# Causal attention layer: the mask of the second pass as TensorE products on the scores, in place of GpSimd selects on the probabilities

## The reference

```python
q, kk, v = [(layernorm(x) @ W.T + b) split into 16 heads of 8 features]
dot = einsum('bhqd,bhkd->bhqk', q, kk)
dot = where(causal, dot, -inf) / sqrt(128)      # key k counts for query q only if k <= q
attn = softmax(dot, axis=-1)
x = x + einsum('bhqk,bhkd->bhqd', attn, v) @ Wo.T + Wo_b
```

## Time and profile before

| What | Value |
|---|---|
| median of 3 runs | 1955.01 us (1954.34 to 1955.83) |
| the profiled execution's own time | 1949.83 us |
| its span in the profile | 1948.0 us |
| mean granted TensorE clock | 0.952 of full speed |
| PE / DVE / ACT / POOL busy | 85% / 72% / 54% / 28% of the span |

### The profile page before, as it was taken

The page is one execution under the profiler, slowest core; times in us unless marked ns, Lnnn a source line. Parts: engine busy times, 40 slices in busy tenths (PEclk is TensorE's granted clock), DMA queues, the critical chain, the costliest instruction groups (busy, mean ns, idle before and its releaser), DMA issues. The chain is left out here.

```text
span 1948.0 us, 37580 instructions
## 1 busy us (share of the span) xinstructions
PE 1659.1 (85%) x12701; PEld 945.7 (49%) x12781; DVE 1400.6 (72%) x4005; ACT 1046.9 (54%) x2110; POOL 543.9 (28%) x739
## 2 busy tenths in 40 slices
PE   3788888889999989996799999999997867688666
PEld 1344434333333333332467776767675645556444
DVE  6788868788788878881467766766664588665887
ACT  1566666666767776775554445445443454343553
POOL 6566656662333333201100000000002323200232
PEclk9899999999999999998899999999999988899798
DMA  5335333332322112200000000000000000000000
GB/s 96 62 64 104 67 64 51 52 50 41 50 51 50 30 32 40 50 2 1 1 2 2 2 2 2 2 3 2 2 2 1 1 1 0 1 1 1 6 16 22
DMA packets 56698, 49.89 MB, mean 26 GB/s; under 512 B 9220, under 2 KB 54468, under 8 KB 56516
## 3 DMA queue, kind: packets, MB, share of 16 engines
q1 hardware_dynamic: 53692, 46.45, 13.1%
q10 hardware_dynamic: 2824, 1.11, 0.4%
HBM read 7.10 MB, written 2.10 MB: 5 GB/s over the span
## 5 line engine op out<-in xcount | busy, mean ns | idle before, releaser
L515 ACT ACTIVATE at_probs<-ps 128x512 f32<-128x512 f32 (+1 forms) x864 | 458.7, 581 | 219.7 <-PE ps L630 162.8
L774 DVE TENSOR_REDUCE at_M<-ps 128x1 f32<-128x512 f32 x512 | 330.1, 682 | 78.7 <-PE ps L606 77.5
L606 PE MATMUL ps<-at_KS,at_QS 96*128 96x512 bf16 (+3 forms) x1024 | 324.2, 348 | 39.9 <-DMA at_KS<-at_splitk 18.2
L630 PE MATMUL ps<-at_QS,at_KS 128*128 128x512 bf16 x944 | 294.0, 342 | 10.7 <-ACT at_probs L515 10.5
L769 DVE CUSTOM_DVE_ANT_0 at_masked<-ps,at_mask_row 128x384 bf16<-128x384 f32 (+3 forms) x512 | 227.1, 484 | 63.2 <-PE ps L606 61.2
L647 PE MATMUL ps<-at_probs,at_V 128*9 128x512 f32 (+3 forms) x2048 | 228.7, 519 | 26.2 <-POOL at_probs L394 19.2
L606 PEld LDWEIGHTS ps<-at_KS,at_QS 96*128 96x128 bf16 x1024 | 94.4, 99 | 253.0 <-DVE at_M L774 105.8
L394 POOL TENSOR_SCALAR_AFFINE_SELECT at_probs<-at_probs 128x128 f32<-128x128 f32 (+2 forms) x352 | 118.1, 346 | 125.2 <-ACT at_probs L515 119.7
L630 PEld LDWEIGHTS ps<-at_QS,at_KS 128*128 128x128 bf16 x1024 | 97.7, 99 | 101.9 <-ACT at_probs L515 30.6
L856 POOL TENSOR_TENSOR la_rstd<-la_vare,mhalf 128x4 f32<-128x4 f32 x16 | 16.1, 1008 | 420.9 <-DVE la_vare L851 420.9
L1267 DVE SCALAR_TENSOR_TENSOR la_phiq<-ps,la_ezq 128x512 f32<-128x512 f32 x64 | 44.1, 690 | 114.9 <-ACT la_ezq L1118 114.9
(11 more groups left out here) (258 smaller groups left out, 3342.6 us busy)
## 6 DMA issues: line engine op xcount, KB each, us to landing
at_QS<-at_splitq SPq DMA_DIRECT2D x288, 64.0 KB
at_KS<-at_splitk SPq DMA_DIRECT2D x279, 64.0 KB
out<-X SPq DMA_DIRECT2D x8, 256.0 KB, 2.3
at_QS<-at_nmT ACTq DMA_DIRECT2D x64, 8.0 KB
at_KS<-at_splitk ACTq DMA_DIRECT2D x9, 64.0 KB
w_raw<-fp_weights SPq DMA_DIRECT2D x1, 560.0 KB, 6.6
w_wv<-L_attn_a_wv SPq DMA_DIRECT2D x1, 512.0 KB, 8.7
w_wo<-L_attn_a_wo SPq DMA_DIRECT2D x1, 512.0 KB, 5.7
```

The source lines that it names most:

```text
L515: act.activation(v(probs[u % 8][:]), v(src), ACT.Exp, scale=layers[layer(n)]["scale"])\
L606: last = pe.matmul(ps[:, FIRST + U % 3, o * stride:o * stride + width], QS[n % 2][0:SHIFT_AT, h, qt * P:(qt + 1) * P], KS[n % 2][0:SHIFT_A ...
L630: last = pe.matmul(ps[:, SECOND + u % 3, c:c + width], KS[n % 2][:, h, kt * P:(kt + 1) * P], QS[n % 2][:, h, 512 - width:512], start=True, ...
L774: v.tensor_reduce(M[gq % 2][:, heads[0]:heads[-1] + 1, qt], src, AX.X, ALU.max).then_inc(max_free, 1)
```

## The change

For each of the 16 products of a causal quad's second pass, a second product follows on TensorE, onto the first 128 columns of the same scores: identity times `mask_kq`, without start, so that it adds -1e30 to the masked scores before ScalarE reads them. The selects on GpSimd and their semaphore are gone, and `sum_keys` waits for ScalarE in both layers. Everything behind line 278 moves up by up to 11 lines.

```diff
-    probs_masked = sem("probs_masked")
...
-        def clear_future(n, q, gq, i):
-            if not causal[layer(n)]:
-                return
-            _, heads, width, stride = second_of(n)[i]
-            u = seconds(gq) + i
-            diagonal = probs[u % 8][:].rearrange("p (h c) -> p h c", c=stride)[:, 0:len(heads), 0:P]
-            g.wait_ge(scores_free, u + 1)
-            g.affine_select(out=diagonal, in_=diagonal, compare_op=ALU.is_ge, fill=0.0, base=0,
-                            pattern=[[0, len(heads)], [1, P]], channel_multiplier=-1).then_inc(probs_masked, 1)
...
-        walk({"spread": root, "turn": turn, "split": split_part, "clear": clear_stacks, "scores": clear_future,
+        walk({"spread": root, "turn": turn, "split": split_part, "clear": clear_stacks,
...
+                masked = causal[layer(n)]
                 last = pe.matmul(ps[:, SECOND + u % 3, c:c + width], KS[n % 2][:, h, kt * P:(kt + 1) * P],
-                                 QS[n % 2][:, h, 512 - width:512], start=True, stop=True)
+                                 QS[n % 2][:, h, 512 - width:512], start=True, stop=not masked)
+                if masked:
+                    last = pe.matmul(ps[:, SECOND + u % 3, c:c + P], core["ident16"][:], core["mask_kq"][:],
+                                     start=False, stop=True)
...
-            pe.wait_ge(probs_masked if causal[layer(n)] else scores_free, seconds(gq) + last_unit(n, kt) + 1)
+            pe.wait_ge(scores_free, seconds(gq) + last_unit(n, kt) + 1)
```

## The result

The change makes the kernel about 1% faster: 1934.71 us in the median of 5 runs (1933.66 to 1941.19) against 1954.34 for the kernel before beside it (5 runs, 1951.58 to 1955.83), a ratio of 0.9906 [0.9889 to 0.9923]. A second set gave 1934.7 and 0.9908 [0.9888 to 0.9929]. The profiled execution took 1933.66 us, its span 1931.9.

What follows compares the result with a forecast made beforehand. No engine was full: TensorE and VectorE wait for each other in turn, TensorE leading an item's first part, VectorE the second. 16.5 us added less 21.3 removed gave about -5 us: 1955.0 to 1950.0 us, range 1941 to 1960.

Steps and rivals of the forecast that it cites:

- What the products cost: Causal second pass, TensorE: 512 added mask products at 0.056 us each, 278 counting, plus 0.9 us at the start: 16.5 us.
- rival 1: Mask products on TensorE pay their weight loads, about 0.091 us each: 5 us slower, 1960 us; chance 0.15.
- The sums: Second-pass sums on TensorE no longer wait for GpSimd's selects: 2.1 us an item, 14 us saved; bounds 0 and 19.2.
- Rival 2: TensorE then waits for VectorE to free first-pass banks, losing half of the 14 us: 1957 us, no change; chance 0.25.
- The start: First sum of the causal stage, at 63 to 67 us, no longer waits for GpSimd: 3.2 us saved; bounds 0 and 3.7.
- The rotation: GpSimd's rotation steps for items 8 and 9 finish earlier, so TensorE waits less: 3.1 us saved; bounds 1 and 3.3.
- VectorE: VectorE's small instructions collide less with GpSimd on shared ports: 1.0 us saved over the stage; bounds -3 and +4.
- The removal as a whole: Taking 352 selects off GpSimd in the causal second pass saves 14 + 3.2 + 3.1 + 1.0 = 21.3 us.
- The sum, carried to the median: Whole kernel: 16.5 - 21.3 = -4.8, say -5 us, taken from the 1955.0 us median of the runs: 1950.0 us.
- Rival 3: VectorE leads more, only a third of the masks lie on the path: 13 us faster, 1942 us; chance 0.12.

Runs made afterwards that it cites:

- a second set: The changed kernel with each mask product made twice, 512 more products with the output unchanged: 1955.01 us, 0.9992 of the kernel before.
- the kernel with neither: The changed kernel without the 512 mask products and without the selects, so the second pass is unmasked: 1922.22 us, 0.9812 of the kernel before.
- the one-quad kernel: The kernel before with mask products instead of selects only in item 0's first quad (16 products): 1949.87 us, ratio 0.9984.
- the first trace of before: The profiled execution of the unchanged kernel before that the prediction was made from: 1949.8 us, item 10's projection to k at 491.8 us.
- The idle selects: The changed kernel with 352 selects put back at their old places in GpSimd's queue, on scratch tiles nobody reads: 1950.43 us, 0.997 of the kernel before.
- the third trace: Another profiled execution of the kernel before, nothing changed, taken after the prediction: item 10's projection to k at 500.5 us.
- the second trace: A further profiled execution of the kernel before, nothing changed, taken after the prediction: item 10's projection to k at 500.5 us.

## Why the prediction was wrong, step by step

The forecast named the right mechanisms and had their sizes wrong. Its miss of 15 us has two halves. In the very trace that it was made from, the change is worth 13.2 us at item 10 and not 4.8: the removal gave 26.6 where 21.3 was counted, and the products took 13.4 where 16.5 was. And from that trace to the typical execution a further 7 us came, which the last step of the sum put at nothing.

- **What the products cost.** About right. 16.5 us forecast; 11 to 18 measured, and 17 and 20 for a second set. In a steady item 1.9 us, which is the prediction's own count: 36 of them less the 3 before ScalarE's copies, times 0.056, is 1.85. With it fell rival 1: eight products last 0.61 us, not 0.75. The Trainium skill (TensorE: Matmul & The Clock Gate, "Back-to-back issue gap") would have 0.081 us for each pair of load and product; the trace does not agree, at 0.056.
- **The sums.** Right in a steady item: 2.1 us forecast for the removal; without products the steps from item to item were 2.15 us shorter, and with them the item is 45.3 us. Over the stage it was taken a little low: no sum waits in the kernel with neither, so all of the 16.0 us are gone where 14 were counted. Rival 2, that the waits move to VectorE's banks, fell: TensorE waited 1.6 us for them in the kernel after, and 7.6 before.
- **The start.** Undersized. I took TensorE's own idle time, 3.2 us; it measured 5.0 in the kernel without products, and 4.4 net in the one-quad kernel where 2.3 was forecast. The bound of 3.7 did not hold it. Most of the further 1.8 us is the clock's: behind its wait, the first trace of before has this (67.1 to 71 us, columns as above),

```profile
67.10:71.00 3.90, 3.88 (x16) 1.16 (x16) 1.48 (x5) 1.09 (x2) 0.99 (x4) 0.56 0.60 86
```

16 products at a clock of 0.56; the kernel with neither has, from the same sum on,

```profile
63.69:67.60 3.91, 3.91 (x31) 1.38 (x31) 2.29 (x9) 2.02 (x4) 2.17 (x2) 0.92 0.60 80
```

The same product stands at 70.55 us in the first and at 65.95 in the second:

```profile
70.55 0.56 PE L630 MATMUL ps<-at_QS,at_KS 128*128 128x256 bf16 x2
```

```profile
65.95 0.38 PE L619 MATMUL ps<-at_QS,at_KS 128*128 128x256 bf16 x2
```

So the kernel with neither is 67.12 - 63.69 = 3.4 us ahead at the sum and 4.6 ahead here, and the clock gives 1.2. The rest came at 83.6 us, where the first trace of before waits 1.0 us for the maxima's transfer and this kernel doesn't, less 0.8 that it lost again on the way to item 2. The one-quad kernel goes the same way: 3.3 ahead, then 4.6, then 5.3, and 4.4 at item 2.
- **The rotation.** 3.1 forecast, 3.8 (both steps in the kernel without products, less two steady items), and 3.5 net of 32 products where these were expected to leave 1.5 to 3. A little small against the first trace of before, and too small by another 1.7 us in the other two, where the clock fell behind this wait.
- **VectorE.** Named, but undersized: one collision of 1.0 us was counted for the whole stage, where the two small instructions are busy 15.7 us longer before than after. The part on the path is smaller: TensorE's waits for the maxima were 2.7 us in the first trace of before and 4.2, all in one, in the third. The idle selects, which bring back collisions and the rotation's wait, cost 12 to 14 us together, and the prediction had 3.1 + 1.0 = 4.1 for the two; of the 13.6 us at the milestone, 6.1 stand behind one wait for the transfer, a term that the prediction did not have. By the Trainium skill (SBUF — State Buffer, "Who interferes with whom") the ports that VectorE shares with GpSimd are an exclusive lock, and the one that comes second waits for the whole instruction of the first; L783's 1.17 us beside a median of 0.177 agree. L783 has both inputs in SBUF, and by the same section such an instruction contends with a GpSimd instruction that reads SBUF without being in one of the modes that the prediction speaks of. L781's 5.55 us in the third trace go further: it ended only with the last of seven GpSimd instructions. What I added was the guess that most of this lies where it doesn't matter.
- **The removal as a whole.** 21.3 us against 26.6 in the stage by the first trace of before. The start (1.8), the sums (up to 2.0) and the rotation (0.7) make most of the difference; the small rest is VectorE's and the transfer's.
- **The sum, carried to the median.** This single step failed most: "The median of the runs is 1955.0, 5.2 us above that execution, and the prediction is for the median: 1955.0 - 5". The difference was taken as the same for every execution. The trace I read was an execution in which TensorE waited 1.0 us at 83.6 us for a transfer; in two others it waited 3.4 and 4.2 there, with the clock at its lower level behind it, and item 10 came 8.7 us later. Of these, 4.0 and 5.2 us were there at item 2, behind these waits, and about 1 of it was made good by item 3. The rest came in the second trace around 268 us (2 us, behind a wait of 1.6 us for VectorE at a clock of 0.57) and in the third at 304 us (4 us, behind L781's collision), and in both behind the rotation's wait (1.7 us). The kernel after has none of these in its two traces, and gains these microseconds as well. By the mean of the traces the removal is 497.6 - 465.3 = 32 us and the change 20.

Rival 3 came nearest in time, 1942, and is refuted as a mechanism: with a third of the masks on the path a steady item would pay 64 x 0.056 / 3 = 1.2 us for its products, and it paid 1.9.

What could have been asked ahead: the median stood 5 us above the execution read, so most executions held a loss that this trace did not show, and the change might remove it too. And the clock behind the wait of the earlier trace rows stood in that very trace.

Not settled: why the maxima's transfer, 8 KB, lands late in some executions, and whether it never does in the kernel after or only didn't in two traces. The products make TensorE ask for it later, which would hide a late landing; that is argued and not shown. In the kernel before the wait comes while SP's stacking transfers run (DMA share 0.60 in the stretch of the 4.17 us wait); the moment of its own landing is not in the trace, and no kernel was run that moved it to another place.

## What to carry to other kernels

A swap is to be costed as one step, in one order, never by terms from different orders: by the runs, adding the products first cost 4 us and the removal then gave 23, and removing first gave 37 and the products then cost 18. Compare such terms item by item before giving a reason: a few us of the difference were waits that covered the products, and the larger part was what the kernel before loses in some executions only. When one engine's short instructions stand in a queue with long ones, count what their presence does to the queue and to neighbours that share a port, not only who waits for them. Read more than one trace before pricing a gain smaller than the spread between executions, and where a wait of 2 to 4 us stands in a stage, look at the granted clock behind it.

## What the runs showed of the hardware

- Products of 128 columns with a weight load each, alternately two different loads and pairwise onto the same place in PSUM, start every 0.05 to 0.06 us, as L630's own groups of four do with one load each onto places of their own (0.056).
- After single waits of 3.2, 4.2 and 3.2 us within busy stretches, the granted clock was at or near the lower of its two levels (0.56, 0.50 and 0.51) for some 4 us, and this cost 1.2, 2.0 and about 2.7 us beyond the waits. After a wait of 2.1 us at one and the same place it was 1.00, 0.50 and 0.60 in three executions of one kernel; after the wait of 1.0 us at 83.6 us it was 1.00.
- A VectorE instruction that takes 0.16 us alone took 5.55 us while GpSimd ran seven instructions without a gap, and ended 0.02 us after the last of them.
- 352 selects of about 0.35 us whose results no instruction reads cost 12 to 14 us of a kernel in which GpSimd, without them, is busy 22% of the span.
- Executions of one and the same kernel differed by 8.7 us at item 10. At item 2, behind one wait for an 8 KB transfer, they differed by 4.0 to 5.2.
